# Longer gather rings in two of three graph aggregations, and a reordered preparation, in a graph and expert-layer kernel

## The reference

```python
agg = lambda h: segment_sum(h[src], dst, 6250)      # sum of gathered rows by destination
h  = layernorm(x)
h  = (1 + eps1) * h + agg(h)                        # first aggregation, 256 wide
h  = relu(relu(h @ W1a + b1a) @ W1b + b1b)
h  = (1 + eps2) * h + agg(h)                        # second, 512 wide (W2a is applied before it)
x  = x + relu(h @ W2a + b2a) @ W2b + b2b
x  = x + slice_attention(layernorm(x))              # softmax over 64 slices, 8 heads
x  = x + relu(batchnorm(dinv * agg(dinv * (layernorm(x) @ W)) + b))   # third, 256 wide
x  = x + experts(layernorm(x))                      # gate over 8, best 2, two layers each
```

## Time and profile before

| | |
|---|---|
| median of 3 runs | 4542.7 us (4540.22 to 4554.68) |
| the profiled execution | 4555.01 us, its span 4553.2 us |
| TensorE / VectorE / ScalarE / GpSimd busy | 3420.3 / 1485.9 / 497.9 / 2790.0 us |
| gathers of the three aggregations | 2538, 2492.6 us busy |
| granted TensorE clock, mean | 0.865 |

### The profile page before, as it was taken

The page is one execution under the profiler, slowest core; times in us unless marked ns, Lnnn a source line. Parts: engine busy times, 40 slices in busy tenths (PEclk is TensorE's granted clock), DMA queues, the critical chain, the costliest instruction groups (busy, mean ns, idle before and its releaser), DMA issues. The chain is left out here.

```text
span 4553.2 us, 40537 instructions
## 1 busy us (share of the span) xinstructions
PE 3420.3 (75%) x12357; PEld 2262.4 (50%) x12359; DVE 1485.9 (33%) x5675; ACT 497.9 (11%) x1162; POOL 2790.0 (61%) x2814
## 2 busy tenths in 40 slices
PE   2388788777878899999999976566566655648996
PEld 2255454444453444444444455445444444438996
DVE  5121112212121443344433445233333343442221
ACT  4010000010110000000000002000000000003432
POOL 3666666666646666667666502666666666635664
PEclk7698888889899999999999987777777877879998
DMA  5333333443349666666666537334334433326887
GB/s 187 91 112 111 109 112 111 120 120 111 109 124 331 192 203 188 193 190 191 192 199 200 176 107 244 107 113 118 119 116 122 121 112 115 115 83 174 204 212 184
DMA packets 321342, 687.10 MB, mean 151 GB/s; under 512 B 58977, under 2 KB 148301, under 8 KB 320855
## 3 DMA queue, kind: packets, MB, share of 16 engines
q0 software_dynamic: 169712, 474.01, 37.8%
q10 hardware_dynamic: 86448, 110.35, 7.2%
q1 hardware_dynamic: 64970, 100.14, 6.7%
HBM read 592.43 MB, written 99.13 MB: 152 GB/s over the span
## 5 line engine op out<-in xcount | busy, mean ns | idle before, releaser
L280 POOL DMA_INDIRECT s_edge_rows<-table,w_src_idx x2538 | 2492.6, 982 | 1271.7 <-issue 716.2
L320 PE MATMUL s_psA<-s_edge_rows,s_onehot 128*128 128x257 f32 (+2 forms) x4932 | 1692.5, 487 | 200.1 <-DMA s_edge_rows<-table,w_src_idx 101.1
L320 PEld LDWEIGHTS s_psA<-s_edge_rows,s_onehot 128*128 128x128 f32 x4932 | 1015.0, 210 | 748.6 <-issue 622.6
L295 DVE TENSOR_SCALAR s_onehot<-w_iota_row,w_dst_l 128x128 f32<-128x128 bf16 x2466 | 531.6, 296 | 28.9 <-PEq L149 15.6
L1994 POOL DMA_INDIRECT acc_rows<-s_y,s_tnode x105 | 166.3, 1583 | 132.5 <-DVE s_y L2117 101.3
L330 PE MATMUL s_psA<-s_edge_rows,s_early 128*128 128x257 f32 (+2 forms) x648 | 224.0, 472 | 13.9 <-issue 11.9
L980 PE MATMUL s_psM<-s_w2a,s_hT 128*128 128x512 f32 x392 | 198.8, 655 | 18.3 <-ACT s_hT L880 11.3
L2142 PE MATMUL s_psU<-s_xT,s_w 128*128 128x128 f32 x1680 | 210.2, 279 | 0.0
L2142 PEld LDWEIGHTS s_psU<-s_xT,s_w 128*128 128x128 f32 x1680 | 201.4, 196 | 0.3 <-issue 0.3
L2152 PE MATMUL s_psD<-moe_w,s_hT 128*128 x840 | 199.5, 381 | 0.0
L974 PE MATMUL s_psM<-s_h1T,s_w1b 128*128 128x512 f32 (+2 forms) x448 | 186.5, 560 | 7.5 <-issue 6.2
(11 more groups left out here) (358 smaller groups left out, 2788.5 us busy)
## 6 DMA issues: line engine op xcount, KB each, us to landing
s_w<-in_L_ffn_W_dram SPq DMA_DIRECT2D x105, 512.0 KB
s_edge_rows<-table,w_src_idx POOLq DMA_INDIRECT x2538
s_swT<-swt_rows SPq DMA_DIRECT2D x12, 1024.0 KB
table<-s_trow ACTq DMA_DIRECT2D x11, 1024.0 KB
own_rows<-s_own ACTq DMA_DIRECT2D x11, 1024.0 KB
s_self_h<-own_rows ACTq DMA_DIRECT2D x11, 1024.0 KB
swt_rows<-s_swT ACTq DMA_DIRECT2D x11, 1024.0 KB
extra_rows<-w_zeros SPq DMA_DIRECT2D x7, 896.0 KB
```

The lines of the kernel that those rows point to most:

```text
L280: pool.indirect_dma_start(self.rows[:, g % self.SLOTS, t, :], None, self.table, bass.IndirectOffsetOnAxis(ap=src_idx[:, at:at + 1], axis=0 ...
L295: last = nc.vector.tensor_scalar(into[:, t, :], iota_row[:, q * P:(q + 1) * P], dst_l[:, at + t:at + t + 1], None, ALU.is_equal)
L320: last = nc.tensor.matmul(banks[b % 2][:, 0:w], self.onehot[:, g % self.AHEAD, t, :], self.rows[:, g % self.SLOTS, t, col:col + w], start= ...
```

## The change

Rings of 14 groups in the first and 16 in the third aggregation. In the preparation: six batches of scales instead of four, their 16 steps issued one by one between the statistics of the two superblocks that follow (the last batch behind all statistics, with the float of `drow` inside it); tile starts after superblock 3, not 1, and the spare steps one to two superblocks later; three casts moved to the front of VectorE's list; TensorE's slice products ahead of the spare tiles; the float of `srow` on GpSimd, not ScalarE; the spare tables ahead of the edge transposes.

```diff
@@ -382,7 +382,8 @@
     S = Scope(stack, "s0")
-    BATCH = ((0, 4), (4, 7), (7, 10), (10, SB + 1))
+    BATCH = ((0, 3), (3, 5), (5, 7), (7, 9), (9, 11), (11, SB + 1))
+    TURNS = 16
     heads_i = S.sb("heads_i", [P, ROWG, 2], I32)
...
@@ -573,6 +575,8 @@
                                         bass.IndirectOffsetOnAxis(ap=start_i[:, g:g + 1], axis=0)).then_inc(sem, 16)
+        pool.wait_ge(s_srow, 16 * GB)
+        pool.tensor_copy(srow_f[:, :, :], srow[:, :, :]).then_inc(s_srowf, 1)
...
@@ -591,7 +595,9 @@
         v.tensor_scalar(row_i[:, :], row_f[:, :], float(P), None, ALU.mult).then_inc(s_row, 1)
...
+        v.tensor_copy(iota_row[:, :], col_i[:, :])
+        v.tensor_copy(spare[:, :], spare_i[:, :])
+        v.tensor_scalar(block_base[:, :], edge[:, 0:NB], -1.0, -float(CENTRE), ALU.mult, ALU.add)
         v.tensor_scalar(member[:, :], member_i[:, :, :].rearrange("p g t -> p (g t)"), lane[0:NB + 1, 0:1], None, ALU.is_equal)
...
@@ -604,20 +610,53 @@
+        def scale_step(i, k):
+            at = slice(BATCH[i][0] * 4, min(BATCH[i][1] * 4, NB))
+            o, x, y = rstd[:, at], var[:, at], tmp[:, at]
+            if k:
+                dve.wait_ge(s_norm, TURNS * i + k)
+            if k == 0:
+                dve.wait_ge(s_dve, aggregated[i])
+                last = v.tensor_scalar(x, mv[:, at, 1], LN_EPS, None, ALU.add)
+            elif k == 1:
+                last = v.tensor_scalar(y.bitcast(I32), x.bitcast(I32), 1, None, ALU.arith_shift_right)
+            elif k == 2:
+                last = v.tensor_scalar(o.bitcast(I32), y.bitcast(I32), -1.0, float(0x5F3759DF), ALU.mult, ALU.add)
+            elif k == TURNS - 1:
+                last = v.scalar_tensor_tensor(shift[:, at], mv[:, at, 0], -1.0, o, ALU.mult, ALU.mult)
+            elif k % 4 == 3:
+                last = v.tensor_tensor(y, o, o, ALU.mult)
+            elif k % 4 == 0:
+                last = v.tensor_tensor(y, y, x, ALU.mult)
+            elif k % 4 == 1:
+                last = v.tensor_scalar(y, y, -0.5, 1.5, ALU.mult, ALU.add)
+            else:
+                last = v.tensor_tensor(o, o, y, ALU.mult)
+            last.then_inc(s_norm, 1)
...
+        aggregated = {}
...
         def stats(sb):
             dve.wait_ge(s_x[sb], 16)
-            for q in range(blocks_of(sb).start, blocks_of(sb).stop):
+            batch = [i for i, (_, end) in enumerate(BATCH) if end in (sb, sb - 1)]
+            turn = 8 * (sb - BATCH[batch[0]][1]) if batch else 0
+            for j, q in enumerate(range(blocks_of(sb).start, blocks_of(sb).stop)):
                 last = v.bn_stats(stat[:, q, :], xl[:, q, 0:D])
+                if batch:
+                    scale_step(batch[0], turn + j)
             ch.link(last)
-            for q in range(blocks_of(sb).start, blocks_of(sb).stop):
+            for j, q in enumerate(range(blocks_of(sb).start, blocks_of(sb).stop)):
                 last = v.bn_aggr(mv[:, q, :], stat[:, q, :])
-            return last
...
-        def scales(i):
-            at = slice(BATCH[i][0] * 4, min(BATCH[i][1] * 4, NB))
-            ch.link(v.tensor_scalar(var[:, at], mv[:, at, 1], LN_EPS, None, ALU.add))
-            rsqrt(ch, rstd[:, at], var[:, at], tmp[:, at])
-            v.scalar_tensor_tensor(shift[:, at], mv[:, at, 0], -1.0, rstd[:, at], ALU.mult, ALU.mult).then_inc(s_norm, 1)
+                if batch:
+                    scale_step(batch[0], turn + size_of(sb) + j)
+            last.then_inc(s_dve, 1)
+            ch.n += 1
+            for i, (_, end) in enumerate(BATCH):
+                if sb + 1 == end:
+                    aggregated[i] = ch.n
+            if batch and turn:
+                for k in range(turn + 2 * size_of(sb), TURNS):
+                    scale_step(batch[0], k)
...
@@ -654,9 +693,6 @@
             dve.wait_ge(s_fs, 1)
-            v.tensor_copy(iota_row[:, :], col_i[:, :])
-            ch.link(v.tensor_copy(spare[:, :], spare_i[:, :]))
-            v.tensor_scalar(block_base[:, :], edge[:, 0:NB], -1.0, -float(CENTRE), ALU.mult, ALU.add)
             v.tensor_tensor(step[0:NS, :], psC[0:NS, 29:30], passing[0:NS, 1:2], ALU.subtract)
...
@@ -667,26 +703,28 @@
                                               ALU.mult, ALU.add)
-            ch.link(last)
+            last.then_inc(s_tables, 1)
+            dve.wait_ge(s_tables, 1)
             v.tensor_scalar(over_b[:, :], over_i[:, :], 1, None, ALU.arith_shift_right)
...
-        after = {0: (), 1: (first_edges, tile_starts), 3: (spare_tiles,), 4: (spare_offsets,), 6: (spare_blocks,)}
+        after = {1: (first_edges,), 3: (tile_starts,), 4: (spare_tiles,), 6: (spare_offsets,), 7: (spare_blocks,)}
         for sb in range(SB + 1):
-            ch.link(stats(sb))
+            stats(sb)
             for do in after.get(sb, ()):
                 do()
-            for i, (_, end) in enumerate(BATCH):
-                if sb == end - 1:
-                    scales(i)
+        for k in range(5):
+            scale_step(len(BATCH) - 1, k)
         dve.wait_ge(s_drow, 16 * GB)
-        v.tensor_tensor(drow_f[:, :, :], drow[:, :, :], base[:, :].unsqueeze(2).to_broadcast([GR, GB, P]), ALU.subtract).then_inc(s_rowf, 1)
+        v.tensor_tensor(drow_f[:, :, :], drow[:, :, :], base[:, :].unsqueeze(2).to_broadcast([GR, GB, P]), ALU.subtract).then_inc(s_drowf, 1)
+        for k in range(5, TURNS):
+            scale_step(len(BATCH) - 1, k)
+        spare_tables()
+        dve.wait_ge(s_sw, 1)
+        v.tensor_tensor(slice_b[:, :], slice_b[:, :], psW[2][:, :], ALU.add)
         dve.wait_ge(s_tr, 2)
         v.tensor_copy(src_idx[:, 0:PERBANK * GR], psT[2][:, 0:PERBANK * GR])
-        v.tensor_copy(src_idx[:, PERBANK * GR:COLS], psT[3][:, 0:COLS - PERBANK * GR]).then_inc(s_trc, 1)
-        dve.wait_ge(s_sw, 1)
-        v.tensor_tensor(slice_b[:, :], slice_b[:, :], psW[2][:, :], ALU.add)
-        spare_tables()
+        v.tensor_copy(src_idx[:, PERBANK * GR:COLS], psT[3][:, 0:COLS - PERBANK * GR])
...
@@ -715,7 +753,7 @@
             nb = size_of(sb)
-            act.wait_ge(s_norm, batch_of(sb) + 1)
+            act.wait_ge(s_norm, TURNS * (batch_of(sb) + 1))
             if sb == SB:
...
@@ -728,11 +766,9 @@
                     ac.activation(slice_w[:, k, :], psW[k][:, :], ACT.Copy)
-        act.wait_ge(s_srow, 16 * GB)
-        ac.activation(srow_f[:, :, :], srow[:, :, :], ACT.Copy).then_inc(s_rowf, 1)
         act.wait_ge(s_tr, 1)
         ac.activation(dst_l[:, 0:PERBANK * GR], psT[0][:, 0:PERBANK * GR], ACT.Copy)
-        ac.activation(dst_l[:, PERBANK * GR:COLS], psT[1][:, 0:COLS - PERBANK * GR], ACT.Copy).then_inc(s_trc, 1)
+        ac.activation(dst_l[:, PERBANK * GR:COLS], psT[1][:, 0:COLS - PERBANK * GR], ACT.Copy)
...
@@ -764,11 +800,6 @@
         last.then_inc(s_st, 1)
-        pe.wait_ge(s_k, 1)
-        mm(psC[0:NS + 1, 21:22], tri[0:NS, 0:NS + 1], extra[0:NS, :], start=True, stop=True)
-        mm(psC[0:1, 24:25], extra[0:NS, :], ones[0:NS, 0:1], start=True, stop=True).then_inc(s_c, 1)
-        pe.wait_ge(s_f, 1)
-        mm(psC[0:NS + 1, 28:30], shifted[0:NS + 1, 0:NS + 1], passing[:, :], start=True, stop=True).then_inc(s_fs, 1)
         pe.wait_ge(s_bd, 1)
...
@@ -777,16 +808,22 @@
         last.then_inc(s_sw, 1)
-        pe.wait_ge(s_rowf, 2)
-        edge_transposes(drow_f, psT[0:2])
-        edge_transposes(srow_f, psT[2:4])
+        pe.wait_ge(s_k, 1)
+        mm(psC[0:NS + 1, 21:22], tri[0:NS, 0:NS + 1], extra[0:NS, :], start=True, stop=True)
+        mm(psC[0:1, 24:25], extra[0:NS, :], ones[0:NS, 0:1], start=True, stop=True).then_inc(s_c, 1)
+        pe.wait_ge(s_f, 1)
+        mm(psC[0:NS + 1, 28:30], shifted[0:NS + 1, 0:NS + 1], passing[:, :], start=True, stop=True).then_inc(s_fs, 1)
         pe.wait_ge(s_passed, 1)
-        pe.wait_ge(s_trc, 2)
         for h in range(2):
...
         last.then_inc(s_over, 1)
+        pe.wait_ge(s_tables, 1)
+        pe.wait_ge(s_drowf, 1)
+        edge_transposes(drow_f, psT[0:2])
+        pe.wait_ge(s_srowf, 1)
+        edge_transposes(srow_f, psT[2:4])
...
@@ -799,7 +836,7 @@
     FIRST, SECOND, THIRD = (0, 1, 2, 3), (5, 7, 9, 11), (14, 16, 18, 20)
-    edges = Edges(S, table1, T1_W, ((0, D + 1),), FP32, GPB - 1)
+    edges = Edges(S, table1, T1_W, ((0, D + 1),), FP32, GPB - 1, slots=14)
     w1a = S.sb("w1a", [P, KD, HID])
...
@@ -1555,7 +1592,7 @@
     CHOICE, RANK, PLACED, USED = 12, 16, (17, 18, 19, 20), (18, 19, 20, 21)
-    edges = Edges(S, table3, D, ((0, D),), FP32, 1, slots=6)
+    edges = Edges(S, table3, D, ((0, D),), FP32, 1, slots=16)
     w = S.sb("w", [P, KD, D])
```

More of the change, by code:

```diff
@@ L477, in build @@
             s_over = S.sem("spare_tables_psum")
+            s_tables = S.sem("spare_tables_read")
             s_drow = S.sem("dst_rows")
             s_srow = S.sem("src_rows")
-            s_rowf = S.sem("edge_rows_float")
-            s_trc = S.sem("edge_transposes_copied")
+            s_drowf = S.sem("dst_rows_float")
+            s_srowf = S.sem("src_rows_float")
```

(2 more changed lines are left out.)

## The result

The changed kernel took 4574.7 us (median of 4 runs, 4569.0 to 4578.6), the kernel before 4544.4 us (4 runs, 4540.2 to 4554.7): ratio 1.0063, 95% interval 1.0046 to 1.0081. It is slower by 0.6%, some 30 us, where the forecast was 10 us faster. The profiled execution has a span of 4570.4 us; that of before, 4553.2 us, was the slowest of its kernel's runs, so the profiles differ by 17 us only.

What follows compares the result with a forecast made beforehand. The prediction took a common 1.44 us a gather, not ring size or TensorE's work, to bound the aggregations. Preparation -14, first end +8, third pace -14 and end +10 gave -10 us: 4545.0 profiled, 4532.7 us median, range 4440 to 4580.

Steps and rivals of the forecast that it cites:

- Preparation, -14: Reordered preparation before the aggregations: its end moves from 82.2 to 68.4 us, a gain of 14 us.
- walk of VectorE: VectorE's preparation work summed in the new order: spare tables done at 64.2 us, transposes and copies at 68.3 us.
- the case of the slow signals: In the preparation, interleaved steps meet slow signals one after another: the gain is only 6 us.
- First aggregation, pace 0: Ring 8 to 14 leaves the pace at 1.44 us a gather: 0 us, with a floor at -145 us.
- a fixed debt of 0.17 us a gather: Each gather leaves about 0.17 us behind; engine signals wait behind it, and GpSimd's ring waits pay it.
- First aggregation, end +8: TensorE up to six groups further behind at the last gather: 0 to +20 us, taken as +8 us.
- Third aggregation, end +10: TensorE up to ten groups further behind at the last gather: 0 to +26 us, taken as +10 us.
- the rival of the longer freeze: First and third aggregations: larger rings delay GpSimd's stops, so TensorE ends later; 4575 up to 4590 us; chance 0.24.
- Third aggregation, pace -14: Ring 6 to 16 removes the third aggregation's excess over the first, 1232 against 1218 us: -14 us.
- The first rival: First and third aggregations: ring slots are the limit, so larger rings remove GpSimd's waits; 4239 or 4384 us; chance 0.20.

Runs made afterwards that it cites:

- e5: The kernel before, unedited, run again in a late session: 4508.8 us.
- e6: The changed kernel, unedited, run again in the same late session: 4550.2 us, ratio 1.0081 to the kernel before.
- e1: The changed kernel with the old rings of 8 and 6, so only the preparation is changed; prompt session: 4087.1 us, 0.9987 of the kernel before.
- e7: Only the preparation changed, rings of 8 and 6, repeated in another prompt session: 0.9986 of the kernel before.
- e13: Only the preparation changed, rings of 8 and 6, repeated once more under prompt signals: 0.9966 of the kernel before.
- e15: The whole changed kernel, unedited, in a prompt session: 4085.0 us, 0.9986 of the kernel before.
- e17: Changed preparation, rings 8 and 6; TensorE waits until the group 6 (first aggregation) or 4 (third) further on has landed; late: 4620.3 us, 1.0245 of the kernel before.
- e18: Changed kernel, rings 14 and 16; TensorE waits until the group 12 (first aggregation) or 14 (third) further on has landed; late: 4667.6 us, 1.0353 of the kernel before.
- the shrinking lead: Changed kernel, GpSimd's permitted lead shrinking to 3 groups towards the end of first and third aggregation; four prompt sessions: 0.9996, 1.0001, 0.9978, 0.9984 of the kernel before.

## Why the prediction was wrong

**Preparation, -14: right.** First gather 84.3 to 72.1 us (-12.2), and 85.1 to 71.4 (-13.7) in e5 and e6. The walk of VectorE holds. The changed kernel's timeline of the stretch where the root steps met the gathers, and then of the walk's end:

```profile
34.57 0.17 DVE L632 TENSOR_SCALAR s_tmp<-s_tmp 128x8 f32<-128x8 f32 x1 [1.17 <-DVE s_tmp L630]
...
40.36 0.43 DVE L644 BATCH_NORM_STATS2 s_stat<-x_xl 128x6 f32<-128x256 f32 x1 [3.29 <-remote]
...
43.06 0.17 DVE L622 TENSOR_SCALAR s_tmp<-s_var 128x8 int32<-128x8 int32 x1 [1.87 <-issue]
```
```profile
65.41 0.62 DVE L709 TENSOR_SCALAR w_over_e<-s_over_f 1x930 int32<-1x930 f32 x1
...
68.60 0.49 DVE L727 CAST w_src_idx<-s_psT 128x334 int32<-128x334 f32 x1
```

The spare tables end at 66.0 us (forecast 64.2) and the copies at 69.1 us (68.3); before, the end was 82.2 us. The small remainder has two sources. One is the case of the slow signals that I had bounded: VectorE waits 1.17, 3.29 and 1.87 us while GpSimd gathers and just behind, and leaves that stretch at 47.1 us where the walk had 45.1; most of this came back, as a superblock with eight steps took 2.4 us (47.11 to 49.52) and not 2.6. The other is a term that I had too small: the spare tables take 3.5 us (62.55 to 66.03), as they had before (78.70 to 82.20), where the walk has 2.2. That the preparation is to blame (theory B) is refuted where signals are prompt, by e1, e7, e13 (0.9966 to 0.9987). Under late signals no run has the preparation alone; there it is the account of the two late pairs, with the growth all in the two tails, that speaks against theory B.

**First aggregation, pace 0: right.** 1216.0 to 1219.8 us, and 1203.4 to 1202.8 us in e5 and e6; ring waits 145 and 146.5 us. **The reason given for it, a fixed debt of 0.17 us a gather, is wrong.** In a prompt session the same gathers leave no debt (e15: 1.27 us, no ring waits), and in e17 they leave more (1.51 us). What repeats in the late runs is that GpSimd stops 57 to 97 times in the first aggregation, for 2.6 to 2.1 us each on average (e5, e18). Why a stop has that length is not shown.

**First aggregation, end +8: the step that failed.** Measured +20.1 and +26.2 us. I had the mechanism, the bound (six groups, 20 us) and the row that TensorE is 35.1 of 45 us busy behind the last gather, and took from it that the work is taken back fast. It is done fast, but none of it is hidden: the tail was mostly TensorE's work before, and what is added makes it longer by as much. **Third aggregation, end +10: the same step.** Measured +32.1 and +31.8 us, over the bound of 26: eleven groups and not ten, and 2.9 us each, not 2.6. In this tail TensorE's work grew by 25.1 us and VectorE's by 19.8 (before, then changed; columns as above):

```profile
4035.00:4086.00 51.00, 23.30 (x76) 16.20 (x75) 24.92 (x127) 2.29 (x7) 1.04 (x3) 0.70 0.12 32
```
```profile
4019.00:4102.00 83.00, 48.37 (x176) 35.67 (x175) 44.73 (x223) 3.56 (x11) 0.93 (x4) 0.75 0.11 31
```

The argument for the low end was that in mid-stage the engines have slack. They have, but under late signals they hardly use it. Two rows of the kernel before, from a stretch in which GpSimd gathers without a stop from 178.98 to 221.06 us:

```profile
192.10 1.54 PE L320 MATMUL s_psA<-s_edge_rows,s_onehot 128*128 128x257 f32 x6 [2.21 <-DMA s_edge_rows<-table,w_src_idx]
...
222.24 0.38 ACT L868 ACTIVATE s_aggT<-s_psT 128x256 f32<-128x256 f32 x1 [38.55 <-remote]
```

At 192.10 us TensorE had caught up, for it waited for gathered rows, and it could go on while GpSimd gathered. Then ScalarE took up a transpose that TensorE had ended at 193.86 us only at 222.24 us, 1.2 us after GpSimd had stopped, and TensorE stood for it. So signals are not barred while GpSimd gathers, but one late signal held the chain here until GpSimd stopped. GpSimd stops when its ring is full, and with a longer ring TensorE is further behind by then. Counted from the timelines every 4 us, the groups whose gathers are issued less the groups that TensorE has summed are 4.8 in the mean of the first and 3.0 of the third aggregation before, 10.6 and 12.4 in the changed kernel, and 1.5 and 1.2 in e15, under prompt signals. The lag thus stood through the whole stage and was not only one of its start. In the third aggregation TensorE waited 18 times for gathered rows before, and twice in the changed kernel, 25.3 of 26.4 us in one of them.

The lag was in the rival of the longer freeze as "the full lag of six and ten groups", priced at 4575 us. That this is the time measured is in part luck: its terms for the two ends, 20 and 26 us, came out at 20.1 and 32.1, and changes elsewhere that it did not have took the excess back. But its mechanism should have been the forecast.

**Third aggregation, pace -14: too large.** -8.5 us, and -1.0 in e5 and e6. I took the difference of 14 us between the third and the first aggregation of the kernel before for the price of the ring of 6. In the first pair it goes from 14.0 to 1.7 us, but in e5 and e6 it is 11.3 and 10.9 us, with ring 6 and ring 16 alike, so the ring isn't shown to be its cause.

**Not foreseen:** the second aggregation, which is unchanged, took 19.6 us less in the changed kernel's profile and 6.9 less in e6. Two executions of the kernel before differ there by as much (1276.2 and 1256.9 us), so I read nothing into it.

**The sum** of the first pair is -12.2 + 3.8 + 20.1 - 19.6 - 0.1 - 8.5 + 33.6 = +17.1 us, the difference of the spans (the last term is the third tail and 1.5 us behind it). Had the second aggregation differed by 6.9 us, as between e5 and e6, it would be +29.8, as the medians are.

**The first rival** (the ring is the limit) falls in both conditions: under late signals the waits stay, under prompt ones there are none to remove. The Trainium skill, Perfetto Trace Analysis, section Identifying Performance Opportunities, says that a repeating gap can mean too few buffers. The measurement decides against that here: 65 gaps with 8 slots and 70 with 14.

**Still open:** each part alone and the shrinking lead under late signals; why some sessions are late; and why under prompt signals only 4 to 13 us of the 17 us earlier start are left at the end. There the second aggregation takes 1137 to 1143 us in the ten runs with the changed preparation that leave it alone, and 1130 to 1136 us in the three with the old one, with the same instructions.

## What to carry to other kernels

A ring lets the producer run ahead, and it also sets how far the consumer may be behind at the last item; where the stage ends in a barrier, count the work that may be left over there and price it in full, unless a row shows the consumer catching up before the end. Read who is short of what before enlarging a buffer: a producer's waits for slots say nothing if the consumer isn't waiting for data. And measure a change of some tenths of a per cent in more than one session, since the sign of this one depended on the condition of the machine.

## What the runs showed of the hardware

**Late and prompt signals.** Of eight sessions (the first comparison and seven of experiments) three were late and five prompt. It isn't fixed to the chip: on chips numbered 3 and 7 one session each was late and one prompt. It isn't the kernel: both unedited kernels ran in either condition. It isn't the gathers' own cost or their transfers: their mean is 984 ns in the changed kernel's late profile and 986 ns in e15, and the queue's packets took 37.5% of 4570.4 us and 42.2% of 4080.3 us, 1714 and 1722 us of sixteen engines' time. The rows of the changed kernel, late, and of e15, prompt:

```profile
q0 software_dynamic: 169712, 474.01, 37.5%
...
L280 POOL DMA_INDIRECT s_edge_rows<-table,w_src_idx x2538 | 2497.1, 984 | 1225.9 <-issue 715.3
```
```profile
q0 software_dynamic: 169712, 474.01, 42.2%
...
L280 POOL DMA_INDIRECT s_edge_rows<-table,w_src_idx x2538 | 2503.3, 986 | 802.1 <-issue 748.4
```

What differs is the idle time before the gathers, 1225.9 against 802.1 us, and with it some 10% of the kernel's time. In the late condition a finished operation of TensorE was seen up to 52 us later, soon after GpSimd had stood still; a delay of 1.2 us in VectorE's own chain (at 34.57 us) ended while GpSimd was gathering. Two more things go with the condition. The mean granted clock of TensorE is 0.861 in the changed kernel's late profile and 0.935 in e15; which follows from which isn't shown, but the delays are idle time of engines and not longer work. And in all late profiles the list of DMA issues has no time of landing for the gathers, where the prompt ones have 2.8 to 3.1 us: the late condition shows in what the profiler records of the signals, too. What causes it none of the runs shows.

**Where it hides.** The Trainium skill, Perfetto Trace Analysis, section Per-instruction lifecycle, says that on every engine neither the wait for a semaphore nor the propagation of its update is inside the time that the profile gives an instruction. The trace agrees: the 52 us stand in no row of their own, only in the idle time in front of L946, with a releaser ("DMA s_drow") that ended long before.
